# Two of three expert weights as the stationary operand, in an attention and mixture-of-experts kernel

## What is computed

```python
B, S, D, F, E = z.shape[0], z.shape[1], 256, 512, 8      # LOOPS = 2, TOP_K = 2
for _ in range(LOOPS):
    z_norm = _rmsnorm(z, norm_w)
    scores = softmax(z_norm @ router_w)
    topk_vals, topk_idx = top_k(scores, TOP_K)            # each row goes to two experts
    ...
    for e in range(E):
        h = silu(z_norm @ w1[e]) * (z_norm @ w3[e])       # 256 -> 512, twice
        mixed = mixed + cw[:, e:e+1] * (h @ w2[e])        # 512 -> 256
    z = z + mixed
```

## Time and profile before

| | |
|---|---|
| median of 3 runs | 1052.9 us (1049.94 to 1055.16) |
| the profiled execution | 1050.72 us |
| its span, first to last instruction | 1049.0 us |
| expert stage, from the first third product to behind the last | 359.3 to 1027.6 us |
| TensorE (PE) busy | 987.4 us, 94% of the span |
| VectorE (DVE), ScalarE (ACT), GpSimd (POOL) busy | 690.5, 574.7, 579.5 us |
| mean granted TensorE clock | 0.989 of full speed |

### The profile page before, as it was taken

The page is one execution under the profiler, slowest core; times in us unless marked ns, Lnnn a source line. Parts: engine busy times, 40 slices in busy tenths (PEclk is TensorE's granted clock), DMA queues, the critical chain, the costliest instruction groups (busy, mean ns, idle before and its releaser), DMA issues.

```text
span 1049.0 us, 22711 instructions
## 1 busy us (share of the span) xinstructions
PE 987.4 (94%) x7246; PEld 678.7 (65%) x7246; DVE 690.5 (66%) x1497; ACT 574.7 (55%) x1122; POOL 579.5 (55%) x755
## 2 busy tenths in 40 slices
PE   7999997989999899999999999999999999999991
PEld 5677776668888577665666765666755566666661
DVE  7889987999999454684435557535469433575557
ACT  4578786668888545433335565335574333333333
POOL 3356686866798755444443366443365544455435
PEclk9999999999999999999999999999999999999996
DMA  9921111000000234334346435338434433665573
GB/s 315 370 68 31 38 32 22 1 6 21 15 26 16 67 107 125 87 69 101 91 109 167 132 98 139 88 106 181 112 111 117 96 91 92 170 173 119 143 187 130
DMA packets 153818, 109.26 MB, mean 104 GB/s; under 512 B 100992, under 2 KB 140544, under 8 KB 153728
## 3 DMA queue, kind: packets, MB, share of 16 engines
q1 hardware_dynamic: 140096, 70.82, 26.5%
q0 software_dynamic: 13632, 37.24, 12.0%
HBM read 54.27 MB, written 31.20 MB: 81 GB/s over the span
## 4 chain that ended last, share of the span: by engine, by line
PE 69%; DVE 9%; POOL 7%; DMA 6%; ACT 4%; issue 3%; SPq 0%; another core or an unknown queue 0%; POOLq 0%; ACTq 0%; DVEq 0%
PE psum_s L930 32%; PE psum_o L2336 16%; PE psum_s L2325 6%; DMA arena<-arena 4%; PE psum_s L1758 3%; PE psum_t L1753 2%; PE psum_t L764 2%; PE psum_o L1804 2%; POOL arena L1057 2%; DVE arena L1489 1%; DMA arena<-in_rope 1%; PE psum_o L1799 1%; PE psum_o L1811 1%; PE psum_s L1735 1%; PE psum_t L2300 1%
## 5 line engine op out<-in xcount | busy, mean ns | idle before, releaser
L930 PE MATMUL psum_s<-w_all,arena 128*128 x1704 | 392.0, 380 | 4.6 <-issue 1.9
L1980 POOL DMA_INDIRECT token_rows<-arena,result_row_of_row x142 | 147.1, 1036 | 296.5 <-ACT arena L2089 291.2
L930 PEld LDWEIGHTS psum_s<-w_all,arena 128*128 128x128 f16 x1704 | 157.8, 98 | 185.2 <-issue 10.9
L2336 PE MATMUL psum_o<-w_all,arena 128*128 x1704 | 209.4, 273 | 9.1 <-DVE arena L2264 8.2
L915 DVE SCALAR_TENSOR_TENSOR arena<-psum_s,gate_scale,arena 128x512 f32<-128x512 f32 x142 | 106.5, 750 | 161.1 <-ACT arena L909 80.6
L2336 PEld LDWEIGHTS psum_o<-w_all,arena 128*128 128x128 f16 x1704 | 164.7, 98 | 54.1 <-issue 15.4
L2264 DVE TENSOR_TENSOR arena<-psum_s,arena 128x512 f16<-128x512 f32 x142 | 97.8, 689 | 132.3 <-ACT arena L2082 114.2
L2089 ACT ACTIVATE arena<-psum_o 128x256 f32<-128x256 f32 x142 | 54.3, 383 | 216.8 <-PE psum_o L2336 214.1
L891 POOL DMA_INDIRECT arena<-sorted_rows,token_of_row x142 | 139.9, 986 | 49.3 <-issue 40.2
L909 ACT ACTIVATE arena<-psum_s,silu_scale 128x512 f32<-128x512 f32 x142 | 97.6, 687 | 108.1 <-PE psum_s L930 56.6
L2082 ACT ACTIVATE arena<-psum_s 128x512 f16<-128x512 f32 x142 | 84.7, 597 | 33.1 <-PE psum_s L2325 22.9
(11 more groups left out here) (326 smaller groups left out, 1364.8 us busy)
## 6 DMA issues: line engine op xcount, KB each, us to landing
arena<-token_rows SPq DMA_DIRECT2D x64, 256.0 KB, 3.1
w_all<-in_L_ffn_w SPq DMA_DIRECT2D x24, 512.0 KB, 10.1
sorted_rows<-w_all SPq DMA_DIRECT2D x24, 256.0 KB
out<-x_sb SPq DMA_DIRECT2D x7, 512.0 KB, 3.1
arena<-arena SPq DMA_TRANSPOSE x172, 2.4
arena<-sorted_rows,token_of_row POOLq DMA_INDIRECT x142
token_rows<-arena,result_row_of_row POOLq DMA_INDIRECT x142
x_sb<-in_L_attn_x SPq DMA_DIRECT2D x1, 2048.0 KB, 14.8
```

The source lines that it names most:

```text
L930: last = nc.tensor.matmul(bank, e_xT[:, u, lx * DC + c, :], w_split[:, bass.ds(e * EW + at, FF)], start=(q == 0), stop=(q == 3 * DC - 1))
L1980: nc.gpsimd.indirect_dma_start(rows, bass.IndirectOffsetOnAxis(ap=targets[:, at : at + 1], axis=0), y_row[:, u, :], None).then_inc(s_sent[ ...
L2336: last = nc.tensor.matmul(psum_e, hT[:, lh, c, :], w_split[:, bass.ds(e * EW + at, D)], start=(q == 0), stop=(q == 3 * FC - 1))
```

## The change

The operands of `inner` change places. A piece of 128 x 128 of `w1` or `w3` is loaded as the stationary operand, and the 128 turned rows move. The result has the hidden values on its partitions, four groups `f` of 128 beside each other in the same bank; the gate then writes `h_all` in the layout that `outer` needs. So `turn_h` and `psum_h` go, and `h_hi` and `h_lo` read `h_all` from SBUF. An `inner` has 4 x 6 matmuls instead of 6. `outer` keeps its matmuls.

The places are kept in registers made by `place`, 16 ahead of each `inner` and 8 ahead of each `outer`. They hold the byte address in full, with the constants that the access pattern would add or take off (`W_BASE`, and `LAST_COLUMN` for the stationary operand) put in beforehand, so that the operand of a matmul is the register and nothing more.

The waits change with it: `inner` of m = 0 waits for the silu of the tile before, m = 1 for its gate; `gate` waits for the `h_lo` before it.

```diff
+        W_BASE, LAST_COLUMN = 16512, 2 * (P - 1)
+        w_bytes = w_all[:, :].bitcast(mybir.dt.uint8)
...
-        h_row = take(FF)
+        h_all = take(FF)
...
+            if s:
+                dve.wait_ge(s_h_lo, s)
-            nc.vector.scalar_tensor_tensor(h_row, psum_b, gate_scale[:, 0:1], silu_a, ALU.mult,
+            nc.vector.scalar_tensor_tensor(h_all, psum_b, gate_scale[:, 0:1], silu_a, ALU.mult,
                                            ALU.mult).then_inc(s_h, 1)
...
+        def place(e, at):
+            return nc.snap(e * (2 * EW) + (2 * at + W_BASE), engines=[mybir.EngineType.PE])
+
+        def stationary(r):
+            return w_bytes[:, bass.ds(r - (W_BASE + LAST_COLUMN), 2 * P)].bitcast(F16)
+
+        def moving(r):
+            return w_bytes[:, bass.ds(r - W_BASE, 2 * D)].bitcast(F16)
+
         def inner(pe, n, e, m):
 
             u = n % UNROLL
+            places = [[place(e, ((m * DC + c) * 2 + lw) * GROUP + f * P + P - 1) for c in range(DC) for lw in range(2)] for f in range(FC)]
             if m == 0:
                 pe.wait_ge(s_turned[u], 16 * (n // UNROLL + 1))
+                if n:
+                    pe.wait_ge(s_silu, n)
+            elif n:
+                pe.wait_ge(s_h, n)
             bank, signal = ((psum_a, s_a), (psum_b, s_b))[m]
-            for q, (c, lx, lw) in enumerate([(c, a, w) for c in range(DC) for a, w in ((0, 0), (1, 0), (0, 1))]):
-                at = ((m * DC + c) * 2 + lw) * GROUP
-                last = nc.tensor.matmul(bank, e_xT[:, u, lx * DC + c, :], w_split[:, bass.ds(e * EW + at, FF)],
-                                        start=(q == 0), stop=(q == 3 * DC - 1))
+            for f in range(FC):
+                for q, (c, lx, lw) in enumerate([(c, a, w) for c in range(DC) for a, w in ((0, 0), (1, 0), (0, 1))]):
+                    last = nc.tensor.matmul(bank[:, f * P : (f + 1) * P], stationary(places[f][2 * c + lw]),
+                                            e_xT[:, u, lx * DC + c, :], start=(q == 0), stop=(q == 3 * DC - 1))
             last.then_inc(signal, 1)
...
             def h_hi(s):
-                act.wait_ge(s_th, s + 1)
-                nc.scalar.activation(hT[:, 0, :, :].rearrange("p c t -> p (c t)"), psum_h, ACT.Copy).then_inc(s_h_hi, 1)
+                act.wait_ge(s_h, s + 1)
+                nc.scalar.activation(hT[:, 0, :, :].rearrange("p c t -> p (c t)"), h_all, ACT.Copy).then_inc(s_h_hi, 1)
...
-                nc.vector.tensor_tensor(hT[:, 1, :, :].rearrange("p c t -> p (c t)"), psum_h,
+                nc.vector.tensor_tensor(hT[:, 1, :, :].rearrange("p c t -> p (c t)"), h_all,
                                         hT[:, 0, :, :].rearrange("p c t -> p (c t)"), ALU.subtract).then_inc(s_h_lo, 1)
...
-            def turn_h(n):
-
-                pe.wait_ge(s_h, n + 1)
-                for c in range(FC):
-                    last = nc.tensor.transpose(psum_h[:, c * P : (c + 1) * P], h_row[:, c * P : (c + 1) * P], ident[:, :])
-                last.then_inc(s_th, 1)
-
             def outer(n, e):
 
+                per = GROUP // D
+                places = [[place(e, ((2 * DC + c // per) * 2 + lw) * GROUP + c % per * D) for lw in range(2)] for c in range(FC)]
                 pe.wait_ge(s_h_lo, n + 1)
                 if n:
                     pe.wait_ge(s_yrow, n)
                 for q, (c, lh, lw) in enumerate([(c, a, w) for c in range(FC) for a, w in ((0, 0), (1, 0), (0, 1))]):
-                    per = GROUP // D
-                    at = ((2 * DC + c // per) * 2 + lw) * GROUP + c % per * D
-                    last = nc.tensor.matmul(psum_e, hT[:, lh, c, :], w_split[:, bass.ds(e * EW + at, D)],
+                    last = nc.tensor.matmul(psum_e, hT[:, lh, c, :], moving(places[c][lw]),
                                             start=(q == 0), stop=(q == 3 * FC - 1))
```

## The result

The changed kernel takes 1099.6 us against 1052.9: 1.0447 times as long, 95% interval 1.0413 to 1.0481. The forecast was 1010, and faster. The profiled execution took 1097.7 us for a span of 1096.0.

A forecast was written before the change was run, and what follows sets the result against it. TensorE was taken to bound the expert stage, with 14.45 of 668.30 us idle. Gains of 37 + 6 - 2 + 1 = 42 us from 1052.9 gave a forecast of 1010 us, core range 998 to 1020, high end 1036.

The forecast's parts named there:

- Transposes go: Turning of gated rows on TensorE: 4 transposes of 111 ns vanish, 0.44 us for each of 142 tiles.
- Pairs at 55.8 ns: First two products: 48 narrow load and matmul pairs take 2.68 us against 2.60, +0.08 us a tile.
- rival 3: First products: narrow pairs' register-addressed loads not hidden, at least 98 ns each, tile 6.01 us, 1289 us; chance 0.05.
- Tile of 3.99 us: Expert tile where TensorE is full: 4.35 - 0.44 + 0.08 = 3.99 us, a gain of 0.363.
- I take hidden: Sequencer's work on places, load and checks, 1.8 to 2.7 us a tile, assumed hidden under TensorE's 3.99 us.
- 8 to 14: Register instructions a tile for all places if several additions share one: 1.1 to 2.0 us plus 0.65.
- Each one addition: Batches of places: 16 + 16 + 8 = 40 places a tile, one addition for each.
- 40p + 0.65 us: Sequencer's need a tile at p per place: hidden under 3.99 us below 83 ns, whole gain gone at 92 ns.
- rival 2: Sequencer sets the pace at the places, between third product and next first half; at 125 ns 1238 us; slower, chance 0.06.
- Its mild form: Sequencer's price a little above 83 ns a place: 1025 to 1050 us; chance 0.17 together with rival 1.
- Waits move: TensorE's waits for silu, gate and subtraction: 1.7 us of cover at the gate, 0.8 us at the third product.
- rival 1: Gate, copy, subtraction and result copy set ordinary tiles: half the gain lost, 1027 us; chance 0.17 with mild rival 2.

The follow-up runs named there:

- e1: Changed kernel with each place made by one addition and no copy; 1008.7 us, 0.9637 of the kernel before.
- a1: The changed kernel itself, unaltered, run again on the third chip; 1100.1 us, 1.0462 of the kernel before.
- a2: e1 repeated on the third chip; 1037.1 us, 0.9864 of the kernel before.
- e7: Changed kernel with the next tile's load, checks and first batch moved ahead of the routing's matmuls and third product; 1183.8 us, 1.1261 of the kernel before.
- e3: Kernel before, operands in their old roles and gated rows still turned, but with places made ahead in batches; 1.0205 of the kernel before.
- b1: The changed kernel itself, unaltered, run again on the fourth chip; 1076.4 us, 1.0273 of the kernel before.
- e5: Changed kernel with the third product's 8 places worked out in two steps, two more records a tile; 1114.4 us, a single run.
- e6: Changed kernel with the copy of each place replaced by a second addition; 1077.6 us, a single run.
- e9: Changed kernel with four additions to a place and no copies, 28 records a tile; 1206.9 us, a single run.
- e2: Changed kernel with all places constant, so every tile takes expert 0's weights; 1002.6 us, 0.9568 of the kernel before.
- e4: Changed kernel's exchange of operands alone, each place worked out at its matmul instead of in batches; 1266.5 us, a single run.

## Why the prediction was wrong, point by point

**Transposes go, 0.44 us: right.** **Pairs at 55.8 ns, 2.68 us: right**, in e1 to the hundredth; rival 3 is out. **Tile of 3.99 us: right for TensorE's work** in a kernel that feeds it: e1 took 0.9637 of the kernel before, and the forecast was 0.959.

**"I take hidden": the step that failed.** The count of records was right (13, "8 to 14"). Three things were wrong around it.

- *The price of one.* I took 0.14 us, from the records of single addresses. A batch record took 0.22 us. In e1 the third product's 8 additions are records of 74 and 42 ns, by the count above six and two additions, so a further pair of additions costs 16 ns. By the same count an addition and a copy take 68 ns and two of each 105, so a further pair of these costs 37 ns. How the 37 divide is open: a copy put to two of each adds 20 (105 to 125), which leaves 17 for an addition where one among additions costs 8, so the mixture may cost and not the copy by itself. "Each one addition" was read off the source and left the copy out: 16 additions are 3 records (e1), and the changed kernel has 5. On one chip copies cost 1100.1 - 1037.1 = 63 us (a1 and a2), more than the forecast's whole gain of 42.
- *The form of the sum.* This is the larger part: 13 x 0.22 + 0.65 = 3.5 us would still be hidden under 3.99. I set 40p + 0.65 us against 3.99, as if the sequencer could run ahead without limit and pairs cost it nothing. The pairs have 0.35 + 0.37 + 0.30 = 1.02 us in the tile taken apart above, a term that I put at nothing without a reason. And it gets 17 pairs ahead. By my formula the measured p = 13 x 0.22 / 40 = 72 ns lies below the 83 ns of rival 2 and is hidden; the tile took 4.5 us. What has to be compared is each run with the pairs in front of it: 1.1 us with 0.95, and 1.84 with what is left behind the third product. e7 (a gap of 1.4 us ahead of the third product by moving a run, with no work added) and e3 (slower with fewer records) show that it is so. The prediction had argued from a batch that stands "in one run before the waits", and that is what made it dear: one run isn't cheaper for standing together, it needs its cover in one piece.
- *The routing's tiles.* The tiles with 12 routing matmuls were 5.62 us and are 6.26. There the load of the number stands behind the 8 short matmuls of the routing (L766), which wait for ScalarE's copy of the turned rows: the copy ends at 590.09 in one such tile and the load starts at 590.16. It then has 3 of the third product's matmuls and these 8 as cover for itself, slow here (583 ns), and for a batch of 1.1 us: 0.80 us idle ahead of L946. I had priced these like all others. In e1 they take 5.2 to 5.5. In b1 the 24 tiles with routing matmuls of this kind lose 10.8 us to the kernel before, of 28.8.

So rival 2 came true in its place and as a kind ("the sequencer sets the pace, at the places"), at a chance of 0.06 and with a point from which it decides that was too high. Its mild form was put among the gains, 1025 to 1050; it gave 1076 on a chip with signals on time.

**"Waits move" and rival 1: small, but not nothing.** 10.5 us are idle for the subtraction (L2280). The four latencies held where signals are on time; the 0.8 us of cover are what e1 lives on where they are not.

**Not foreseen at all: the late signals**, 1.0273 without and 1.0462 with them, so some 20 us of the changed kernel's 49 on the third chip (an estimate, from two chips). The profile of the changed kernel that stands at the head shows them too.

**Signs.** "No more than 14 records" was fulfilled and misleading: the number was no measure of their time. "Gaps before L930's loads that nothing released" was the right sign of rival 2, and the page shows it as 64.9 us of issue.

## What to carry to other kernels

Before narrowing matmuls whose addresses come from registers, price the sequencer by runs: how long is each run of register work, loads and checks, and how many microseconds of matmuls can be handed out ahead of it (17 pairs here, 0.95 us of narrow ones). Put runs behind the longest matmuls, split them, and count the records that one line of address arithmetic became: 16 places were 5 records 0.22 us apart with an addition and a copy each, and 3 records 0.133 us apart with one addition each. Taking the copies out, which also made 8 records of 13, turned a loss of 4.6% into a gain of 1.4% on one chip. Measure variants beside each other on one chip before comparing them.

## What the runs showed of the hardware

- The sequencer of TensorE was never more than 17 load and matmul pairs ahead of the array, in the kernel before, the changed one, e1, e5, e6 and e9 and their repeats.
- Register records of a batch took 74 ns by median (42 to 88) where places were made by additions alone (e1, e6, e9) and 160 (67 to 191) with a copy beside each addition (changed kernel). Either way some 60 ns more passed to the next record's start (74 to 133, 160 to 220).
- On two chips of four, and in the changed kernel's run at the head, the signal behind 24 narrow pairs with batched register addresses often reached the waiting engine more than 0.5 us after the last pair's start and not 0.26 (silu in the changed kernel: in 106 of 135 tiles, longest 2.48 us). The third product's (256 columns) was on time in all but 1 to 7 tiles of a run (0.31 us from the last matmul's start to the copy), and that of 512 columns in e3 in all but 4 (0.42 us). On the other two chips it was never late. The attention's narrow pairs that signal at their end (12 in a row, L1817 in the kernel before) are read by ScalarE, where it stood free (2 to 5 groups of a run), 0.26 us after the last one's start on all four chips (0.34 once, in a2). Which property of the kernel brings it out stays open: e2 and e4, without batches, never met such a chip. Whether the products themselves end late or only their signal is open too; the next group's starts, 56 ns later, speak for the signal.
